# First attention of a hybrid layer: shifts sent straight into the query tile, stack rows reordered, and a maximum pass that runs eleven steps ahead instead of twelve

## The reference

```python
qkv = x @ w_qkv.T                       # 16 heads, two sub-heads of HD = 4 each
def sdpa(qi, ki):
    s = jnp.einsum('bnhd,bmhd->bhnm', qi, ki) * scale
    p = jax.nn.softmax(s, axis=-1)
    return jnp.einsum('bhnm,bmhe->bhne', p, v)
a1 = sdpa(q[:, :, :, 0], k[:, :, :, 0])
a2 = sdpa(q[:, :, :, 1], k[:, :, :, 1])
o = a1 - lam * a2
o = _rms_norm(o, sub_norm_w, EPS) * (1.0 - LAMBDA_INIT)
```

## Time and profile before

| what | value |
|---|---|
| median of 3 runs | 1095.35 us (1095.05 to 1095.57) |
| profiled execution | 1094.11 us |
| its span (first to last instruction) | 1092.0 us |
| PE busy | 1001.1 us, 92% |
| DVE busy | 956.8 us, 88% |
| ACT busy | 890.1 us, 82% |
| POOL busy | 487.9 us, 45% |
| first maximum / last exponential of the first attention | 36.4 / 653.8 us |

### The profile page before, as it was taken

How to read it: one execution, slowest core, us unless ns; L and a number is a source line. 1 busy time by engine, 2 the same in 40 slices (tenths; PEclk the granted TensorE clock), 3 DMA queues, 4 the chain that set the end, 5 groups by cost and what they waited for, 6 DMA issues and landing times.

```text
span 1092.0 us, 21659 instructions
## 1 busy us (share of the span) xinstructions
PE 1001.1 (92%) x8016; PEld 513.8 (47%) x8016; DVE 956.8 (88%) x1186; ACT 890.1 (82%) x1466; POOL 487.9 (45%) x893
## 2 busy tenths in 40 slices
PE   6389999999999999999999999999899899999998
PEld 3022222222222222222232337777777777777876
DVE  7799999999999999999999948787877987687665
ACT  5179999999999999999999986777776776677775
POOL 3363545454545555554456466433224332432431
PEclk9579999999999999999999999999999999999999
DMA  8911110111011101110110017665577476757773
GB/s 278 303 33 46 52 50 4 50 51 51 3 51 51 51 4 51 51 34 20 51 51 22 2 27 192 152 163 135 143 175 176 134 172 167 192 145 176 187 192 101
DMA packets 80472, 108.90 MB, mean 100 GB/s; under 512 B 23536, under 2 KB 33520, under 8 KB 80368
## 3 DMA queue, kind: packets, MB, share of 16 engines
q1 hardware_dynamic: 66336, 100.98, 35.1%
q10 hardware_dynamic: 14032, 6.55, 2.3%
HBM read 95.57 MB, written 11.93 MB: 98 GB/s over the span
## 4 chain that ended last, share of the span: by engine, by line
DVE 51%; PE 29%; ACT 7%; issue 5%; DMA 4%; POOL 2%; ACTq 1%; SPq 1%; DVEq 0%; POOLq 0%
DVE NEGMAX L1060 43%; PE PS L1451 8%; PE PS L1453 7%; PE PS L1452 7%; DVE HL L1109 2%; PE PS L1353 2%; ACT HH L943 2%; DVE HF L1101 2%; ACT PR L855 2%; DMA RAWU<-in_L_ffn_W_up_dram 2%; PE PS L1326 1%; PE PS L1232 1%; ACT L950 1%; POOL WUL L627 1%; DMA GATE<-gate_d 1%
## 5 line engine op out<-in xcount | busy, mean ns | idle before, releaser
L1060 DVE TENSOR_REDUCE NEGMAX<-PS 128x1 f32<-128x1024 f32 x512 | 584.5, 1208 | 9.9 <-PE PS L1289 9.2
L855 ACT ACTIVATE PR<-PS 128x512 f32<-128x512 f32 x1024 | 538.7, 600 | 36.5 <-PE PS L1326 24.2
L1353 PE MATMUL PS<-PR,VG 128*32 128x256 f32 (+1 forms) x3840 | 321.2, 406 | 17.5 <-ACT PR L855 2.0
L1326 PE MATMUL PS<-QB,KB 32*128 32x512 bf16 x1024 | 260.1, 387 | 3.0 <-DMA QB<-shift_d 1.7
L1289 PE MATMUL PS<-KA,QA 32*128 32x512 bf16 x1024 | 204.4, 397 | 30.9 <-DVE NEGMAX L1060 22.5
L1101 DVE TENSOR_TENSOR HF<-PS,GATE 128x1024 f32<-128x1024 f32 x128 | 156.2, 1221 | 73.8 <-ACT PS L950 72.0
L950 ACT ACTIVATE PS<-PS 128x1024 f32<-128x1024 f32 x128 | 129.3, 1010 | 93.5 <-PE PS L1453 93.1
L1326 PEld LDWEIGHTS PS<-QB,KB 32*128 32x128 bf16 x1024 | 75.0, 91 | 239.2 <-ACT PR L855 138.1
L943 ACT ACTIVATE HH<-HF 128x1024 fp32r<-128x1024 f32 (+1 forms) x136 | 139.7, 1028 | 19.5 <-DVE HF L1101 18.7
L1109 DVE TENSOR_TENSOR HL<-HF,HH 128x1024 fp32r<-128x1024 f32 (+1 forms) x104 | 129.8, 1248 | 12.5 <-ACT HH L943 12.5
L767 POOL TENSOR_TENSOR HL<-HF,HH 128x1024 fp32r<-128x1024 f32 (+1 forms) x32 | 70.2, 2194 | 155.0 <-ACT HH L943 155.0
(11 more groups left out here) (186 smaller groups left out, 970.6 us busy)
## 6 DMA issues: line engine op xcount, KB each, us to landing
GATE<-gate_d SPq DMA_DIRECT2D x256, 256.0 KB, 4.1
QA<-q_stack SPq DMA_DIRECT2D x64, 128.0 KB, 2.6
QB<-q_stack SPq DMA_DIRECT2D x16, 256.0 KB, 3.0
KB<-k_stack SPq DMA_DIRECT2D x16, 256.0 KB, 3.0
KA<-k_stack SPq DMA_DIRECT2D x60, 64.0 KB, 2.4
q_stack<-PARTS SPq DMA_DIRECT2D x12, 256.0 KB, 4.3
k_stack<-PARTS SPq DMA_DIRECT2D x12, 256.0 KB, 4.4
RAWU<-in_L_ffn_W_up_dram ACTq DMA_DIRECT2D x4, 512.0 KB, 11.9
```

The costliest lines, as they stand in the source:

```text
L855: nc.scalar.activation(PR[:, s % PRING, r, :], PS[:, SCORE_BANK[n], :], ACT.Exp, scale=SCALE_A).then_inc(p_ready, 1)
L1060: nc.vector.tensor_reduce(NEGMAX[:, hs % 2, col:col + 1], PS[:, e:e + 2, :].rearrange("p b n -> p (b n)"), axis=AX_X, op=ALU.max, negate=T ...
L1326: mm(PS[:, SCORE_BANK[n], :], KB[strip, u, mt * P:(mt + 1) * P], QB[strip, u, half * BANK:(half + 1) * BANK], start=True, stop=True).then_ ...
L1353: last = mm(PS[STRIP * r:STRIP * (r + 1), 7, cols], VG[:, u, mt, r // 2, :], PR[:, s % PRING, r, cols], start=mt == 0, stop=mt == TB - 1 a ...
```

## The change

Four things change together.

- **Order of the rows.** A strip was slot by slot (slot c, then the 4 rows d of the vector); it is now d by d, with 8 slots in each (r, d, c). Slots 6 and 7 hold zeros or ones. The stacks in DRAM have the same layout, so the repeated parts are written by one transfer each: 8 a batch entry.
- **The shift rows** are now slot 7 of each d: every eighth partition of QB. GpSimd's four operations write SHP in the order attention, part, tile (with a fourth part that stays zero, set once at the start), so that the transposed copy SHT, now 64 rows, has its rows in the order in which they belong in QB. One transfer per half sends it there. shift_d and the wait between write and read are gone.
- **LEAD** is 11 instead of 12. The steps of the transposition, the copy and the first score stay (`shift_at` is not changed).
- **The side work** in the last steps of the attention is one step later (NQ - 11 to NQ - 2).

```diff
-STACK_WRITES = 16 * 2 * (len(Q_SLOTS) + 1)
+SLOTS = STRIP // HD_A
+SHIFT_SLOT = SLOTS - 1
+STACK_WRITES = 16 * 2 * 4
-LEAD = 12
+LEAD = 11
...
-    NQ - 8: [("x_T", ("f", 0))], NQ - 7: [("affinity", 0)], NQ - 6: [("top", 0)], NQ - 5: [("sum", 0)], NQ - 3: [("gate_T", 0)],
+    NQ - 7: [("x_T", ("f", 0))], NQ - 6: [("affinity", 0)], NQ - 5: [("top", 0)], NQ - 4: [("sum", 0)], NQ - 2: [("gate_T", 0)],
...
-                    for c in places:
-                        rows = stack[b * GPB:(b + 1) * GPB, :, HD_A * c:HD_A * (c + 1), :].rearrange("g r d n -> (g r) d n")
-                        sp.dma_start(rows, src).then_inc(st_w[b], 16)
+                    step = places[1] - places[0] if len(places) > 1 else 1
+                    rows = stack[b * GPB:(b + 1) * GPB].rearrange("g r d c n -> (g r d) c n")[:, places[0]:places[-1] + 1:step, :]
+                    sp.dma_start(rows, src.unsqueeze(1).to_broadcast([P, len(places), SEQ])).then_inc(st_w[b], 16)
...
                 u, hs = s % 2, 2 * s + half
+                if half == 0:
+                    sp.wait_ge(sh_w, 16 * (s + 1))
                 sp.wait_ge(sht_ok, hs + 1)
-                sp.dma_start(shift_d[half].rearrange("a r (t n) -> (a r t) n", n=P), SHT[:, half, :]).then_inc(sh_w, 16)
-
-                sp.wait_ge(sh_w, 48 * s + 16 * (half + 2))
-                for r in range(R):
-                    lo = STRIP * r + SHIFT_ROW
-                    sp.dma_start(QB[lo:lo + 3, u, half * BANK:(half + 1) * BANK], shift_d[half, :, r, :]).then_inc(sh_r, 16)
+                sp.dma_start(QB[SHIFT_SLOT:P:SLOTS, u, half * BANK:(half + 1) * BANK], SHT[:, half, :]).then_inc(sh_r, 16)
...
-                nc.gpsimd.tensor_tensor(SHP[:, u, 0:w], NEGMAX[:, u, :], ZERO[:], op=ALU.add).then_inc(sh_split, 1)
+                nc.gpsimd.tensor_tensor(SHP[:, u, :, 0, :], top, ZERO[:].rearrange("p (r t) -> p r t", r=R), op=ALU.add).then_inc(sh_split, 1)
...
             link(nc.gpsimd.memset(ZERO[:], 0.0))
+            link(nc.gpsimd.memset(SHP[:], 0.0))
             shift_parts(0)
...
-                    dve.wait_ge(sh_w, 48 * (hs // 2 - 1) + 16 * (hs % 2 + 2))
-                nc.vector.tensor_copy(SHT[:, hs % 2, :], PS[0:3 * SHIFTS, SCORE_BANK[n], 0:P // 2].bitcast(BF16)).then_inc(sht_ok, 1)
+                    dve.wait_ge(sh_r, 16 * (hs - 1))
+                nc.vector.tensor_copy(SHT[:, hs % 2, :], PS[0:4 * SHIFTS, SCORE_BANK[n], 0:P // 2].bitcast(BF16)).then_inc(sht_ok, 1)
```

More of the change, by code:

```diff
@@ L364, in hybrid_layer @@
         OTS = sb("OTS", [P, 2, BANK], where=attn)
-        SHP = sb("SHP", [P, 2, 3 * SHIFTS], BF16, where=attn)
-        SHT = sb("SHT", [3 * SHIFTS, 2, P], BF16, where=attn)
+        SHP = sb("SHP", [P, 2, R, 4, SHIFTS // R], BF16, where=attn)
+        SHT = sb("SHT", [4 * SHIFTS, 2, P], BF16, where=attn)
         ZERO = sb("ZERO", [P, SHIFTS], where=attn)
@@ L397, in hybrid_layer @@
         PS = ctx.enter_context(nc.psum_tensor("PS", [P, 8, BANK], F32))
[L400 to L401 removed]
+        q_stack = nc.dram_tensor("q_stack", (NG, R, HD_A, SLOTS, SEQ), BF16, kind="Internal").ap()
+        k_stack = nc.dram_tensor("k_stack", (NG, R, HD_A, SLOTS, SEQ), BF16, kind="Internal").ap()
         gate_d = nc.dram_tensor("gate_d", (2 * NCH, E, BANK), F32, kind="Internal").ap()
         mixed_d = nc.dram_tensor("mixed_d", (BATCH, S0, HD_B, HEADS_B, S1), F32, kind="Internal").ap()
[L404 removed]
         ld_x = [sem(f"ld_x{c}") for c in range(NCH)]
@@ L469, in fill_shift_rows @@
                 for stack, fill in ((q_stack, ZEROS), (k_stack, ONES)):
-                    rows = stack[b * GPB:(b + 1) * GPB, :, SHIFT_ROW:STRIP, :].rearrange("g r s n -> (g r) (s n)")
-                    sp.dma_start(rows, fill[:].unsqueeze(1).to_broadcast([P, 2, SEQ])).then_inc(st_w[b], 16)
+                    rows = stack[b * GPB:(b + 1) * GPB].rearrange("g r d c n -> (g r d) c n")[:, len(Q_SLOTS):SLOTS, :]
+                    sp.dma_start(rows, fill[:].unsqueeze(1).to_broadcast([P, SLOTS - len(Q_SLOTS), SEQ])).then_inc(st_w[b], 16)
             def write_parts(b, part):
@@ L497, in load_strips @@
             def load_strips(stack, tile, u, g, there):
-                sp.dma_start(tile[:, u, :], stack[g].rearrange("r s n -> (r s) n")).then_inc(there, 16)
+                sp.dma_start(tile[:, u, :], stack[g].rearrange("r d c n -> (r d c) n")).then_inc(there, 16)
             def load_max(u, g, keys=True):
@@ L639, in shift_parts @@
                 pool.wait_ge(m_free, ITEM["max", TB * hs + TB - 1, 1] + 1)
-                u, w = hs % 2, SHIFTS
-                nc.gpsimd.tensor_tensor(SHP[:, u, 0:w], NEGMAX[:, u, :], ZERO[:], op=ALU.add).then_inc(sh_split, 1)
+                u = hs % 2
+                top, rest = (t.rearrange("p (r t) -> p r t", r=R) for t in (NEGMAX[:, u, :], SHR[:]))
+                nc.gpsimd.tensor_tensor(SHP[:, u, :, 0, :], top, ZERO[:].rearrange("p (r t) -> p r t", r=R), op=ALU.add).then_inc(sh_split, 1)
                 pool.wait_ge(sh_split, (4 * hs + 1))
-                nc.gpsimd.tensor_tensor(SHR[:], NEGMAX[:, u, :], SHP[:, u, 0:w], op=ALU.subtract).then_inc(sh_split, 1)
+                nc.gpsimd.tensor_tensor(rest, top, SHP[:, u, :, 0, :], op=ALU.subtract).then_inc(sh_split, 1)
                 pool.wait_ge(sh_split, (4 * hs + 2))
-                nc.gpsimd.tensor_tensor(SHP[:, u, w:2 * w], SHR[:], ZERO[:], op=ALU.add).then_inc(sh_split, 1)
+                nc.gpsimd.tensor_tensor(SHP[:, u, :, 1, :], rest, ZERO[:].rearrange("p (r t) -> p r t", r=R), op=ALU.add).then_inc(sh_split, 1)
                 pool.wait_ge(sh_split, (4 * hs + 3))
-                nc.gpsimd.tensor_tensor(SHP[:, u, 2 * w:3 * w], SHR[:], SHP[:, u, w:2 * w], op=ALU.subtract).then_inc(sh_split, 1)
+                nc.gpsimd.tensor_tensor(SHP[:, u, :, 2, :], rest, SHP[:, u, :, 1, :], op=ALU.subtract).then_inc(sh_split, 1)
                 pool.wait_ge(sh_split, (4 * hs + 4))
@@ L771, in _ @@
                 side(where)
-                if where == NQ - 11:
+                if where == NQ - 10:
                     heads_norm(2 * NG - 3)
@@ L1321, in scores @@
                 if q % TB == 0 and p == 0:
[L1322 removed]
+                    pe.wait_ge(sh_r, 16 * (s // TB + 1))
                 bank_free(n)
```

16 lines of the change are left out of this document (6 added, 10 removed).

## The result

| | before | after |
|---|---|---|
| median of 6 runs | 1095.46 us (1094.93 to 1095.94) | 1118.51 us (1117.68 to 1119.61) |
| ratio | | 1.0213, 95% interval 1.02 to 1.0225 |
| profiled execution, its span | 1094.11 us, 1092.0 us | 1119.51 us, 1117.6 us |
| first exponential | 62.9 us | 64.2 us |
| end of the last maximum | 625.1 us | 648.7 us |

A forecast was written before the change was run, and what follows sets the result against it. VectorE, with no slack in the steady attention, was taken as the bound; +16.8 - 2.4 + 2.4 - 0.9 + 0.8 = +16.7 us on 1094.1 gives 1110.8, the median 1.2 above: forecast 1112 us, range 1103 to 1121.

The forecast's parts named there:

- The stall: VectorE waits 0.59 us (0.58 for the sum) at the shift copy in half groups 2 to 30: +16.8 us.
- The links: Last maximum to GpSimd's start 0.15 us, its operations 1.10, to the transposition 0.11, to VectorE's copy 0.28: T + 1.64.
- The forecast's own case: Stall of 0.5 to 0.7 us with the other terms as bounded: 1108 to 1117 us, chance 0.60.
- rival 2: TensorE's 0.76 us wait at the tile spreads to ScalarE or adds to VectorE's stall: 1118 or 1134 us; chance 0.17.
- Rival 1: The late transfer bounds and the tile's wait is covered: 1092.4 or 1095 us; faster 0.06, within 0.2% 0.03.
- rival 4: GpSimd's chain or the hand-over is quicker, stall 0.3 us, +8.7 instead of 16.8: 1104 us; chance 0.10.
- Rival 3: The direct transfer lands above 3.9 us from its issue; at 5.6, +49 us: 1161 us; chance 0.04.
- The stack writes: 24 transfers become 12 with the same bytes, DMA engines bound by bytes from 20 to 29 us: 0 (-0.6 to +1.0).
- The start: GpSimd holds half groups 0 and 1, copy 1 at 77.3 to 77.4 after 33 maxima instead of 35: +2.4 us.
- One step fewer at the end: One step fewer of scores between the last maximum and the last exponential, 2.39 us a step: -2.4 us.
- GATE: After the attention, side work one step later makes the first GATE loads 1.3 us late: +0.8 us (0 to +2.4).
- The direct transfer: One SBUF transfer of 1.4 us replaces two trips into QB, returning part of VectorE's 1.4 us idle time: -0.9 us.

The follow-up runs named there:

- run 1: Changed kernel with 12 steps of lead again and the side work at its old steps: 1097.65 us (ratio 1.0023).
- run 5: Changed kernel with the tile's transposition and copy both one step later: 1097.55 us (1.0029).
- run 6: Changed kernel with one more small GpSimd operation, its result unused, in each shift chain: 1129.41 us (1.0319).
- run 4: Changed kernel with VectorE's shift copy behind the second maximum of its step instead of the first: 1114.4 us (1.0176).
- run 2: Changed kernel with the stack writes split, one transfer per slot: 1113.99 us (1.0174).
- run 7: Changed kernel with 12 steps of lead and one stack write per slot: 1095.61 us (1.0005).
- run 11: Changed kernel with only GpSimd's bias sum of X moved behind the second shift chain: 1115.31 us (1.0193).
- run 12: Changed kernel with one stack write per slot and the bias sum of X behind the second shift chain, transposition at its old step: 1114.92 us (1.0189).
- run 8: Changed kernel with transposition and copy one step later, one stack write per slot, bias sum of X behind the second shift chain: 1094.74 us (1.0001).
- run 9: Changed kernel, transposition one step later, w_up load behind group 0's, its casts in pieces in half groups 3 to 11, bias sum late: 1094.95 us (1.0007).
- run 3: Kernel before with 11 steps of lead and the side work moved along, nothing else: 1121.35 us (1.0245).

## Why the prediction was right, and where it was off

**The stall: right, in mechanism and size.** Forecast 0.58 us a half, measured 0.607: 0.52 idle at the copy, and the other 0.08 because the copy and the maximum ahead of it no longer overlap. The links (0.15, 1.10, 0.11, 0.28) came from the earlier trace rows and were each met within 0.04; the forecast counted the last two from the weight load of the transposition, the text above from its matmul, and their sum is 0.40 in both traces. Runs 1 and 5 show that it goes when the lead or the tile's step is changed, run 6 that it grows with GpSimd's chain.

**The time: in the range, but not by its own case.** The forecast's own case reached to 1117. The measured 1118.51 lies above it, in the part of the range that was kept for rival 2, and rival 2 is not what happened. The terms that follow are what carried it there.

**Rival 2, that the stall spreads: no.** TensorE waits 0.82 us (forecast 0.76), but the spacing is 18.94, so VectorE's stall covers it. Run 4 shows that it was just below the surface. Rival 1 falls by the spacing, rival 4 as well. Rival 3 falls by the landing of the new transfer:

```profile
DMA to landing us min/median/max: 1.8/2.5/3.1
```

(all transfers into QB, 100 to 600 us; the direct ones alone have a median of 1.8.) It was taken as 1.4, the row of the write; it is a third more, and still 2 us below the 3.9 from which it would be late. No score waits for more than 0.4 us. Beside rival 1 the prediction cites a fixed 2.0 us for every transfer, from "Anatomy of one DMA" on the page "DMA: Bandwidth & Descriptors" of the Trainium skill. That section gives it for transfers issued by GpSimd, and SyncE issues those here. By the rows here the whole time to landing is less, 1.4 and 1.8 us, and the terms of the forecast do not rest on it.

**The stack writes: the step that failed.** They were put at 0, bounds -0.6 and +1.0, because bytes bound the stretch from 20 to 29 us. That stretch has only batch entry 0. Those of entry 1 run beside the load of w_up, and their merging costs 4.5 us in the changed kernel (run 2). The same edit is worth 2.0 with lead 12 (run 1 against 7, intervals that overlap) and 0.4 with the bias sum late (run 11 against 12), so its size is not firm; that the start is late with merged writes is shown by all six of their profiles. The argument looked at the writes' own rate, not at who shares the engines with them and who waits for that one. The trace of before had it: 21.85 us of ScalarE's wait for RAWU, and the chain WUH, WUL, X, shifts. That the two queues share the 16 DMA engines is what the shares above show; the page "DMA: Bandwidth & Descriptors" of the Trainium skill, section "Queues, rings and completion order", says that an engine takes turns between queues packet by packet. By that a queue with small packets beside one with large ones would lose whenever the other has more in hand. The landing times, and that SyncE issues its writes sooner, fit that, but it is argued, not shown: no run here varied the size of a piece.

**The start: +2.4 met in size, partly by luck, and incomplete as a sum.** Run 12 against run 8 has 2.5 for it. But the forecast had half group 1 held by the bias sum of X, and in run 12 that sum is out of the way: the chain waits 3.96 us for VectorE instead, and the 2.5 are VectorE's waits at the first two copies. On top came 2.8 for the late weights, and 2.1 for the clock after the standstill. In run 1 TensorE stands still at the same place for no less time, but its clock is at 0.50 only from 81 to 84 us, and the next copy is 1.0 late instead of 2.1; that speaks for the clock and not the standstill as what costs there. Run 11 takes 3.0 us away by moving one operation. Copy 0 was forecast at about 57.0 and came at 55.70, because GpSimd's setup, which waits for the last stack write, began at 50.65 instead of 53.26; copy 1 was late all the same.

**One step fewer at the end: -2.4 forecast, +0.2 measured.** Three parts. With a late tile the tail is 26.5 to 26.6 us (runs 5, 8, 9), 2.1 less than before. Half group 31 has the tile's wait of 0.82 us too, though no maxima are behind it; that makes 27.37 (runs 2, 3, 11, 12). The forecast counted only VectorE there, but TensorE's scores stand behind the tile. The changed kernel has 28.87, and its clock fell once more:

```profile
660.00:665.00 5.00, 5.00 (x33) 1.77 (x31) 1.65 (x4) 2.36 (x5) 3.76 (x7) 0.70 0.00 0
```

TensorE is busy all 5 us but ScalarE only 2.36. Run 4 has such a stretch (0.66, tail 28.86), run 6 as well (0.50, tail 30.46), runs 2, 3, 11 and 12 none. Why it falls in some and not in others was not settled: run 4 does without VectorE's wait, and has it.

**GATE: +0.8 forecast.** From the last exponential to the end the ten kernels with lead 11 have a mean of 440.6 us, the four with lead 12 a mean of 439.1: +1.5, inside the bounds of 0 and +2.4. These are single executions, which scatter by 1 us and more. The wait that was forecast is there, though; in the changed kernel VectorE now stands still for GATE ahead of the first two operations that use it, where the earlier trace rows have no wait ahead of the first:

```profile
682.41 1.23 DVE L1100 TENSOR_TENSOR HF<-PS,GATE 128x1024 f32<-128x1024 f32 x1 [0.64 <-DMA GATE<-gate_d]
684.65 1.22 DVE L1100 TENSOR_TENSOR HF<-PS,GATE 128x1024 f32<-128x1024 f32 x1 [1.01 <-DMA GATE<-gate_d]
```

**The direct transfer: -0.9 forecast, -1.3 measured** between the copies. In the time of the whole kernel it can't be told from nothing with lead 12 (run 7), and is worth 7 with lead 11 (run 3). The forecast held that "this transfer hardly reaches the bound" without saying at which lead.

With the 2.8 and 2.1 us of the start in the sum, the forecast would have been 1117. The tail (2.6 more than forecast), the end (1.1) and the stall (0.8) would add 4.5, the vanished gaps take off 0.4; that makes 1121, and the profiled executions were 2.35 us further apart than the medians.

## What to carry to other kernels

- Shortening a lead by one step saved one step at one end at most, and is paid at every place where the consumer then stands closer behind the producer than the chain between them is long. Before giving up lead, write down that distance (here three maxima to one, 1.05 us) and the length of the chain that must fit (1.64 us), and move the consumer along with the lead.
- When transfers are merged, ask who else is on the DMA engines in that stretch, and follow what waits for the other queue through every list, not only the transfer's own reader.
- Two waits at one place hide each other. Removing one shows what it is worth only when the other goes too (4 us against 21, of which 17.6 are the stall).
